# Experts in row tiles of 512, down stage one step behind the up stage, optional 128-row blocks past row 1024, first weight pieces loaded during attention

## What is computed

```python
x = x + _L0_xcond_ref(_layernorm(x), ctx_2048, ctx_2048, itok_B_779_1933)
x = x + _L0_ffn_ref(_layernorm(x), L0_ffn_Wg, L0_ffn_w1, L0_ffn_w2)

# attention: 16 batches, 8 heads of 32 channels, 512 queries and keys
attn = jnp.einsum('bhdq,bhdk->bhqk', qh, kh)
attn = jax.nn.softmax(s * attn, axis=-1)          # s depends on k_length
out = jnp.einsum('bhqk,bhdk->bhdq', attn, vh)

# experts: E = 8, K = 2, C = 1280, d = 512, D_FF = 2048
probs = jax.nn.softmax(xr @ Wg, axis=-1)
gate_vals, expert_idx = jax.lax.top_k(probs, K)
...                                               # rows of each expert, in order, up to C
h = jax.nn.relu(jnp.einsum('ecd,edf->ecf', dispatched, w1))
expert_out = jnp.einsum('ecf,efd->ecd', h, w2)
out = jnp.einsum('ks,ksm->sm', combine_weights, rerouted)
```

## Time and profile before

| | us |
|---|---|
| median of 3 runs | 2404.62 |
| lowest, highest | 2404.28, 2413.33 |
| the profiled execution's own time | 2401.92 |
| its span | 2400.2 |
| PE busy | 2251.4 (94%) |
| DVE, ACT, POOL busy | 939.2, 740.3, 490.4 |

### The profile page before, as it was taken

How to read it: one execution, slowest core, us unless ns; L and a number is a source line. 1 busy time by engine, 2 the same in 40 slices (tenths; PEclk the granted TensorE clock), 3 DMA queues, 4 the chain that set the end, 5 groups by cost and what they waited for, 6 DMA issues and landing times. The chain is left out here.

```text
span 2400.2 us, 37555 instructions
## 1 busy us (share of the span) xinstructions
PE 2251.4 (94%) x14066; PEld 1784.1 (74%) x14067; DVE 939.2 (39%) x1817; ACT 740.3 (31%) x1261; POOL 490.4 (20%) x690
## 2 busy tenths in 40 slices
PE   3899999999948987899999999999999999999998
PEld 1445555555428876799898899889989989988997
DVE  5577877777534112211331242241241123224111
ACT  1566666666623102211221231131231122113110
POOL 3134343434230333400010110010010001001001
PEclk9899999999969988899999999999999999999999
DMA  9987887878325112411331241241151024023100
GB/s 130 150 162 172 164 177 158 177 157 186 98 88 180 48 37 69 138 23 27 88 88 27 57 134 18 65 131 22 34 163 22 18 57 129 18 65 100 21 18 11
DMA packets 115927, 217.62 MB, mean 91 GB/s; under 512 B 24527, under 2 KB 24535, under 8 KB 115800
## 3 DMA queue, kind: packets, MB, share of 16 engines
q1 hardware_dynamic: 85536, 174.78, 30.8%
q0 software_dynamic: 22240, 37.92, 8.2%
q10 hardware_dynamic: 8064, 3.82, 0.9%
HBM read 113.93 MB, written 68.29 MB: 76 GB/s over the span
## 5 line engine op out<-in xcount | busy, mean ns | idle before, releaser
L1144 PE MATMUL ps_h<-xhi,w1hi 128*128 128x256 f32 x2240 | 640.2, 286 | 34.3 <-issue 13.5
L1146 PE MATMUL ps_h<-xhi,w1lo 128*128 128x256 f32 x2240 | 641.2, 286 | 10.7 <-issue 10.2
L1145 PE MATMUL ps_h<-xlo,w1hi 128*128 128x256 f32 x2240 | 639.2, 285 | 8.4 <-issue 8.3
L982 ACT ACTIVATE hhi<-ps_h 128x512 fp32r<-128x512 f32 x280 | 167.4, 598 | 1191.0 <-PE ps_h L1146 1139.0
L1144 PEld LDWEIGHTS ps_h<-xhi,w1hi 128*128 128x128 f32 x2240 | 429.4, 192 | 41.7 <-issue 38.1
L1145 PEld LDWEIGHTS ps_h<-xlo,w1hi 128*128 128x128 f32 x2240 | 428.7, 191 | 13.7 <-issue 12.5
L1146 PEld LDWEIGHTS ps_h<-xhi,w1lo 128*128 128x128 f32 x2240 | 428.1, 191 | 10.3 <-issue 10.3
L1159 PE MATMUL ps_y<-w2hi,hhi 128*128 128x512 f32 x1072 | 425.8, 397 | 0.0
L1161 PE MATMUL ps_y<-w2hi,hlo 128*128 128x512 f32 x1072 | 423.1, 395 | 0.0
L1160 PE MATMUL ps_y<-w2lo,hhi 128*128 128x512 f32 x1072 | 423.1, 395 | 0.0
L1055 DVE SCALAR_TENSOR_TENSOR hlo<-ps_h,hhi 128x512 fp32r<-128x512 f32 x280 | 193.6, 691 | 554.9 <-ACT hhi L982 525.0
(11 more groups left out here) (127 smaller groups left out, 1812.7 us busy)
## 6 DMA issues: line engine op xcount, KB each, us to landing
raw<-in_L_ffn_w SPq DMA_DIRECT2D x128, 512.0 KB
xin<-dispatched SPq DMA_DIRECT2D x40, 528.0 KB, 3.8
kst<-khi SPq DMA_DIRECT2D x64, 256.0 KB
qst<-qhi SPq DMA_DIRECT2D x64, 256.0 KB
xt<-in_x SPq DMA_DIRECT2D x32, 256.0 KB, 3.6
ct<-in_ctx SPq DMA_DIRECT2D x32, 256.0 KB, 3.4
kst<-klo SPq DMA_DIRECT2D x32, 256.0 KB
qst<-qlo SPq DMA_DIRECT2D x32, 256.0 KB
```

Of the source, the lines that this page charges most:

```text
L982: nc.scalar.activation(hhi[:, 2 * f:2 * f + 2, :], ps_h[f % 4][:], ACT.Relu).then_inc(hhi_ready, 1)
L1144: nc.tensor.matmul(to, w1hi[:, c, fs], xhi[:, c, :], start=(c == 0), stop=False)
L1145: nc.tensor.matmul(to, w1hi[:, c, fs], xlo[:, c, :], start=False, stop=False)
L1146: last = nc.tensor.matmul(to, w1lo[:, c, fs], xhi[:, c, :], start=False, stop=(c == NC4 - 1))
```

## The change

Everything is in the expert stage, but for three weight loads.

- **Tiles.** T is 512, two tiles per expert, always run in full (1024 rows). Rows past 1024 run as up to two blocks of 128 rows (`end_tile`), each behind a branch, between the two tiles. Their up stage has 128 moving columns.
- **Up and down interleaved.** `up(n, f)` makes one block of 128 hidden units for 512 rows (12 matmuls of 512 columns, one bank of `ps_h`, now 3 banks), and `down(n, f - 1)` follows: 4 row blocks x 3 matmuls into 4 banks `ps_y`. `hhi` and `hlo` hold two blocks in place of 16.
- **Turning rows.** `x_turn` turns a quarter (4 transposes) after blocks 2, 5, 8 and 11 of the tile before, into one bank `ps_x`; `xhi`, `xlo` are double. The first tile is turned at once, into `ps_y`.
- **Weights.** A piece holds what two hidden blocks need, of w1 (1 KB runs) or w2 by turns; NRAW is 3. SP loads pieces 0 to 2 at the end of its attention program. Cuts of expert e + 1 stand in tile 1 of expert e.
- **Loads.** A tile is 4 DMAs of 264 KB; the rows past 1024 go to `xend`. SP's list is written out.
- **POOL.** `fill_spare(e + 1)` stands at the start of expert e: 10 DMAs per expert. `turn` is gone. A tile's output takes 4 DMAs in a row, and both end blocks' DMAs are issued whether the blocks ran or not.
- **No loops.** All engines' programs are straight, with branches for the end blocks alone.

```diff
-T = 256
-TILES = CAP // T
+T = 512
+TB = T // P
...
-NRAW = 4
+NRAW = 3
+XAT = (2, 5, 8, 11)
+ENDAT = 13
...
+            for i in range(NRAW):
+                sp.dma_start(raw_view(raw, i), weight_piece(w1, w2, 0, i)).then_inc(raw_ld[i], 16)
```

SP's list, and POOL's:

```diff
+                    k = PIECES * e + i
+                    if k >= NRAW:
+                        sp.wait_ge(w_ready, k - NRAW + 1)
+                    sp.dma_start(raw_view(raw, k), weight_piece(w1, w2, e, i)).then_inc(raw_ld[k % NRAW], 16)
+
+            def tile_in(n):
+                if n >= 1:
+                    sp.wait_ge(xt_done, NC4 * n)
                     sp.wait_ge(gates_kept, n)
                     sp.wait_ge(ids_kept, n)
-                sp.dma_start(xin[:], disp_t[bass.ds(n, 1)].rearrange("n p h w -> (n p) h w")).then_inc(xin_ld, 16)
...
-            weights(0, range(12), True)
+                if n >= 2 and n % 2 == 0:
+                    sp.wait_ge(spare_st, (n // 2) * (16 * FILLS))
+                for b in range(TB):
+                    sp.dma_start(xin[:, b, :], disp_b[n // 2, TB * (n % 2) + b]).then_inc(xin_ld, 16)
...
+            tile_in(0)
+            weights(0, range(NRAW, 8))
             tile_in(1)
-            weights(0, range(12, PIECES), True)
-            with sp.Fori(1, E) as e:
-
-                weights(e, range(NRAW), False)
-                with sp.Fori(2, TILES + 1) as t:
-                    sp.wait_ge(spare_st, e * (16 * FILLS))
-                    tile_in((e - 1) * TILES + t)
-                weights(e, range(NRAW, 12), False)
-                tile_in(e * TILES + 1)
-                weights(e, range(12, PIECES), False)
-            with sp.Fori(2, TILES) as t:
-                tile_in((E - 1) * TILES + t)
+            end_in(0)
+            weights(0, range(8, PIECES))
+            for e in range(E - 1):
+                weights(e + 1, range(NRAW))
+                tile_in(2 * e + 2)
+                weights(e + 1, range(NRAW, 12))
+                tile_in(2 * e + 3)
+                end_in(e + 1)
+                weights(e + 1, range(12, PIECES))
...
-            keep_ids(0, 0)
-            for t in range(TILES):
-                keep_ids(t + 1, (t + 1) % TILES)
-                add(t, t)
-                if t == 0:
-                    fill_spare(1)
-                elif t < TILES - 1:
-                    fill_spare(2 * t)
-                    fill_spare(2 * t + 1)
...
+            keep_ids(0)
+            keep_ids(1)
+            for e in range(E):
+                keep_end_ids(e)
+                if e + 1 < E:
+                    fill_spare(e + 1)
+                    keep_ids(2 * e + 2)
+                add(2 * e)
+                add_end(e, 0)
+                add_end(e, 1)
+                if e + 1 < E:
+                    keep_ids(2 * e + 3)
+                add(2 * e + 1)
```

DVE's list (ACT's has the same places):

```diff
+                for t in range(2):
+                    n = 2 * e + t
+                    for f in range(NF):
+                        if not (t == 1 and f == 0):
+                            low(n, f)
+                        if t == 0 and f == 0 and e >= 1:
+                            y_out(n - 1)
+                        if n == 0 and f % 2 == 0 and f < NF - 2:
+                            cut(0, f + 2)
+                            cut(0, f + 3)
+                        if f in XAT and n + 1 < N:
+                            x_low(n + 1, XAT.index(f))
+                        if f == 3 and n + 1 < N:
+                            keep_gates(n + 1)
+                        if t == 0 and f == ENDAT:
+                            end_low(e, 0)
+                            keep_end_gates(e)
+                        if t == 0 and e >= 1 and f == 1:
+                            cut(e, PIECES - 2)
+                            cut(e, PIECES - 1)
+                        if t == 1 and e + 1 < E and f % 2 and f >= 3:
+                            cut(e + 1, f - 3)
+                            cut(e + 1, f - 2)
+                    if t == 0:
+                        with dve.If(rows > 2 * T):
...
+                            y_out(n)
+                            low_end(e, 0)
+                            y_out_end(e, 0)
...
+                            low(n + 1, 0)
+                        with dve.Else():
...
+                            low(n + 1, 0)
+                            y_out(n)
```

PE's stages and its list:

```diff
+            def up(n, f):
+                k = NF * n + f
...
+                if f == 0:
+                    pe.wait_ge(xlo_ready, NC4 * (n + 1))
+                if n % 2 == 0 and f % 2 == 0:
+                    pe.wait_ge(w_ready, PIECES * (n // 2) + f + 1)
+                if k >= 3:
+                    pe.wait_ge(h_ready, k - 2)
+                to = ps_h[k % 3][:]
+                for c in range(NC4):
+                    nc.tensor.matmul(to, w1hi[:, c, fs], xhi[n % 2][:, c, :], start=(c == 0), stop=False)
+                    nc.tensor.matmul(to, w1hi[:, c, fs], xlo[n % 2][:, c, :], start=False, stop=False)
+                    done = nc.tensor.matmul(to, w1lo[:, c, fs], xhi[n % 2][:, c, :], start=False, stop=(c == NC4 - 1))
+                done.then_inc(h_done, 1)
...
+            def down(n, f):
+                k = NF * n + f
+                pe.wait_ge(h_ready, k + 1)
+                if n % 2 == 0 and f % 2 == 0:
+                    pe.wait_ge(w_ready, PIECES * (n // 2) + f + 2)
+                for b in range(TB):
...
+                    bs = slice(P * b, P * b + P)
+                    nc.tensor.matmul(ps_y[b][:], hhi[k % 2][:, bs], w2hi[:, f, :], start=(f == 0), stop=False)
+                    nc.tensor.matmul(ps_y[b][:], hhi[k % 2][:, bs], w2lo[:, f, :], start=False, stop=False)
+                    done = nc.tensor.matmul(ps_y[b][:], hlo[k % 2][:, bs], w2hi[:, f, :], start=False, stop=(f == NF - 1))
...
+            def up_end(e, half, f):
+                fs = slice(P * f, P * f + P)
...
+                to = ps_h[f % 3][:, 0:P]
+                for c in range(NC4):
+                    nc.tensor.matmul(to, w1hi[:, c, fs], ehi[:, c, :], start=(c == 0), stop=False)
+                    nc.tensor.matmul(to, w1hi[:, c, fs], elo[:, c, :], start=False, stop=False)
+                    done = nc.tensor.matmul(to, w1lo[:, c, fs], ehi[:, c, :], start=False, stop=(c == NC4 - 1))
+                done.then_inc(eh_done[half], 1)
```

```diff
+                for t in range(2):
+                    n = 2 * e + t
+                    for f in range(NF):
+                        if not (t == 1 and f == 0):
+                            up(n, f)
+                        if f in XAT and n + 1 < N:
+                            x_turn(n + 1, XAT.index(f))
+                        if t == 0 and f == ENDAT:
+                            end_turn(e, 0)
+                        if f:
+                            down(n, f - 1)
+                        elif t == 0 and e >= 1:
+                            down(n - 1, NF - 1)
+                    if t == 0:
+                        with pe.If(rows > 2 * T):
+                            down(n, NF - 1)
+                            end_tile(e, 0)
+                            with pe.If(rows > 2 * T + P):
...
+                            up(n + 1, 0)
+                        with pe.Else():
...
+                            up(n + 1, 0)
+                            down(n, NF - 1)
+            down(N - 1, NF - 1)
```

More of the change, by code:

```diff
@@ L876, in _, with weights @@
         def _(sp):
[L877 removed]
+            def weights(e, pieces):
                 for i in pieces:
[L879 to L889 removed]
```

548 lines of the change are left out of this document (278 added, 270 removed).

## The result

The changed kernel takes 2340.49 us (median of 4 runs, 2338.22 to 2345.55) where the kernel before takes 2406.03 beside it: a ratio of 0.9725, 95% interval 0.9698 to 0.9752. It is faster by 2.75%, some 66 us; 2339 was forecast. The profiled execution spans 2343.8 us, against 2334.1 in the sum; it was the longest of the four.

The account below looks back on a forecast made before the run. Bound by PE's work (busy 94%) and its holes, mainly 53 us in expert 0. Sum 726 + 1.5 + 1431.6 + 33.3 + 101 + 13.5 + 0 + 8 + 19.2 = 2334.1, plus 4.4: 2339; range 2325 to 2422.

Parts of the forecast that it names:

- Starvation: PE's holes beside POOL's spare-row store bursts in expert 0: 53 us lost before, 0 with seven bursts of 10.
- upper bound of 29: Most that seven bursts of 10 stores could cost PE, from 4.1 us lost at the earlier burst of 10.
- Narrow matmuls: End blocks' up matmuls with 128 moving columns: 0.109 us each, three end blocks at 33.6, together 101 us.
- rival A: End blocks: narrow matmuls cost as much as 512-column ones, 65 or 71 us more, 2404 to 2410; chance 0.38.
- Up and down: Main tiles of the expert stage: 6144 matmuls of 512 moving columns at 0.233 us, 1431.6 us.
- Rival C: Expert stage: a handshake late in every block, 0.1 us each is 26 us, 0.3 is 77; 2365 to 2420; chance 0.10.
- Turning: Transposing rows on PE: 68 groups of 4 transposes at 0.49 us each, 33.3 us.
- The second tile's wait: PE at expert 0's third block end waits for the second tile's load: 11.5 us idle plus 2 lower clock, 13.5.
- The start: PE's first up matmul of the expert stage, behind tile load, transposes and last high and low part: at 726 us.
- Branches: Eight row-count loads and eight branches over the end blocks: 8 us, 0 to 15.
- The tail: End of kernel behind PE: four output DMAs in a row, 3 x 5.0 + 4.4, given as 19.2 us.
- The claimed origin: Gain's sources: about 53 us starved stretches, 20 main tiles, 8 end blocks, 10 boundaries, less 13.5 and 7.

Follow-up runs that it names:

- the moved load: Changed kernel with expert 0's second tile and end-row loads ahead of weight pieces 5 to 7 in SyncE's queue: 2328.1 us, ratio 0.9666.
- the spread-store kernel: Kernel before, with its 70 spare-row stores issued by ones and twos behind the output additions of each expert's tiles 0 to 2: 2350.7 us, ratio 0.9754.

## Why the prediction was right

The direction, the size and the forecast's mechanism held: 2339 was forecast and 2340.5 measured. Against its own sum of 2334.1 the span is 9.7 us longer, and that is several misses of both signs. That the median came within 1.5 us is in part luck: I added 2.7 us for a median above the profiled execution, and here the profiled one lies 5.1 above the median.

- **Starvation, 0 instead of 53 us**: right, and so was its reasoning, that what PE has in hand lasts twice as long as before and longer than a burst. The runs give the numbers: 73 to 87 matmuls in hand, and stores by ones and twos that free the kernel before of 49 us. That it is instructions that PE lacks was said and isn't shown. Of the 53 us, some 1.4 were something else: the fourth stretch is the first up stage of expert 1, and its first 15 matmuls ran at half clock behind a wait of 2.2 us for DVE's `xlo`. Its upper bound of 29 for seven bursts of 10 would have been too low for the kernel before (40 us), since it took the loss from one stretch that ran at full clock. The margin is thin: a burst of 20 costs 9 to 11 us.
- **Narrow matmuls, 0.109**: 0.107 measured; rival A, which had as large a chance as the forecast, is out. One record stands for each call, unlike the plain f32 ones of the earlier trace rows. The estimate from the Trainium skill's page "TensorE: Matmul & The Clock Gate", section "Back-to-back issue gap" (about 81 ns), isn't borne out by these reduced-type matmuls; the row of the transposes, 99 ns, was nearer. The three end blocks took 98.8 us of the forecast 101, stops apart.
- **Up and down, 1431.6**: 24 matmuls take 5.59 us, which makes 6144 of them 1431. Rival C is out: no hole at any block.
- **Turning, 33.3**: too high. A group takes 0.36 us and the twelve matmuls behind it 0.06 more (2.86 instead of 2.80): 0.42, about 28 in all.
- **The second tile's wait, 13.5**: 9.3 us, and 2.4 at half clock behind it, 12 in all (0.4 for the transposes and 2.0 for the next 12 matmuls, 4.83 instead of 2.80). The prediction's own figures gave a wait of 10.9 (749 - 738.1), where it wrote 11.5. It came at 743, not 738, because the stage began later. The cause was the one named, as the moved load shows.
- **The start, 726**: 730.09. The attention part ended 4.0 us later in this execution (the tile's load was issued at 718.83, has 714.81), and the term counted from the issue was right. Over the traces here the first up matmul scatters from 722.9 to 730.7 with nearly the same code, so I count this miss as chance.
- **Branches, 8**: the term that was mis-sized most. The stops are 9.4, the half clock behind them 5.8 and the five cheap skips 0.9 together: 16. I had the price of a stop too low (1.89 of the earlier trace rows against 3.05 to 3.3) and forgot that a stop is paid twice, by the clock.
- **The tail, 19.2**: 25. The additions are 5.7 us apart, not 5.0 as I had put it for additions without `turn`: 2.1 more. The span ends 8.1 us behind the last one's issue, not 4.4: 3.7 more. (The prediction's 3 x 5.0 + 4.4 is 19.4, too, not 19.2.) Both prices came from the earlier trace rows, and those were additions of rows that are mostly or wholly spare; the last ones of the changed kernel carry full tiles. The queue of the additions (packets, MB, share) from 2390.4 to 2395.8 and from 2395.8 us to the end before, and from 2330 to 2335.5 us in the changed kernel:

```profile
q0 software_dynamic: 144, 0.09, 14.2%
q0 software_dynamic: 144, 0.00, 1.6%
```

```profile
q0 software_dynamic: 144, 0.26, 36.7%
```

  They landed 4.6, 2.8 and 4.7 us after their issue. What the last 3.5 us of the changed kernel's span go to isn't shown.

The claimed origin was too generous to the tiles: "20 main tiles, 8 end blocks, 10 boundaries, less 13.5 and 7" is 17.5 us, and the spread-store kernel leaves 10.5; the branches (8 more) and the tail (6 more) took more than that back, the transposes (5 less) returned some.

## What to carry to other kernels

Where an engine that is fully busy shows waits that nothing releases, look at what the other queues issue in that stretch, and count how many instructions it got through before the first hole: that number against the burst's length tells whether a smaller burst, or fewer and larger instructions, is enough. A taken branch and a late load cost more than their hole on TensorE where it returned at half clock (holes of 3 us and more here; those under 1 us kept the full clock); put the branch behind work that is already queued, with the frequent case first. And before crediting a restructuring with its whole gain, remove the suspected cause alone in the old kernel: here moving 70 stores gave 49 of 59 us.

## What the runs showed of the hardware that I had not expected

- TensorE ran on for 73 to 87 matmuls after a burst of stores began, in 14 of 15 bursts, whether they had 256 or 512 columns; then it got 0.5 to 1.5 a us. In time, its reserve was some 9 to 11 us at 256 columns (once 15.3) and 17.6 us or more at 512. It starved so in loops too, in a stretch of 104 us in which no instruction queue moved a packet.
- A jump over the unused second block cost 3.05 to 3.3 us of a bare TensorE. With 12 matmuls of 512 columns queued ahead, a jump over both blocks cost up to 0.4 us in the changed kernel and up to 0.7 in the others, and the one behind an end block 0.7 to 1 where its branch was turned round.
- A reduced-type matmul with a new 128 by 128 weight takes 0.107 us with 128 columns and 0.105 with 64; with 512 columns 0.233.
- Four additions of full rows into DRAM that wait for each other are 5.7 us apart; issued without waits, 1.85. One of spare rows alone lands after 2.8 us instead of 4.6 to 4.9.
